# Four-pass graph network on one core: buffers reused after ScalarE's count of evictions instead of TensorE's count of sums

## What is computed

```
e = edges, s = src[e], d = dst[e]
1  score = exp(clip(sum_over_head(K[s] * Q[d] / sqrt(12) * E[e]), -5, 5));  x += sum_e(V[s] * score) / (sum_e(score) + 1e-6)
2  mean = sum_e(x[s]) / deg;  peak = max_e(relu(x @ Wpool + b)[s]);  x += leaky_relu(bn(x, mean) + bn(x, peak))
3  x += (sum_e(x[s] * ci[s]) * cj[d]) @ W + b
4  y = sum_e((x @ W)[s] * w[e]);  x += layernorm(y + bias) * gamma + beta
```

## Time and profile before

| what | us |
|---|---|
| median of 3 runs | 5184.86 (5175.81 to 5187.15) |
| profiled execution, first to last instruction (its own time is given by this span alone) | 5246.3 |
| GpSimd busy | 3200.4 (61%) |
| TensorE busy, matrix products | 2714.9 (52%) |
| VectorE busy | 1982.1 (38%) |
| ScalarE busy | 1353.8 (26%) |
| gathers of pass 1, first to last | 42.0 to 1411.5 |
| gathers of pass 2 | 1471.2 to 2718.4 |
| gathers of pass 3 | 2809.2 to 3998.5 |
| gathers of pass 4 | 4024.9 to 5214.0 |

### The profile page before, as it was taken

One profiled execution on the slowest core, in us unless ns is written; L12 is line 12 of the kernel. 1 busy time (PEld: TensorE's weight loads), 2 busy tenths in 40 slices (PEclk: granted clock), 3 DMA queues, 4 the chain that ended last, 5 costly groups with the idle time before them and its releaser, 6 DMA issues.

```text
span 5246.3 us, 56090 instructions
## 1 busy us (share of the span) xinstructions
PE 2714.9 (52%) x15042; PEld 2473.5 (47%) x15042; DVE 1982.1 (38%) x4498; ACT 1353.8 (26%) x4318; POOL 3200.4 (61%) x3366
## 2 busy tenths in 40 slices
PE   6666676666756666566683543332334333333334
PEld 6666676666645555556552432222224222222234
DVE  3555545555655555555554111111113221122124
ACT  1121112222333333333343321211112121111113
POOL 4555555556356666666646666666665666666664
PEclk7676666767777777777785555555555555555555
DMA  7655555555433333333321111111112111111111
GB/s 193 156 142 140 148 137 139 149 143 144 125 94 85 81 84 83 82 83 83 83 60 42 35 35 35 35 35 35 35 35 46 35 36 34 35 35 34 35 35 44
DMA packets 337349, 409.90 MB, mean 78 GB/s; under 512 B 212224, under 2 KB 248691, under 8 KB 336957
## 3 DMA queue, kind: packets, MB, share of 16 engines
q0 software_dynamic: 133120, 245.58, 19.7%
q1 hardware_dynamic: 203933, 160.75, 11.7%
HBM read 386.26 MB, written 19.77 MB: 77 GB/s over the span
## 4 chain that ended last, share of the span: by engine, by line
another core or an unknown queue 32%; PE 19%; DVE 15%; POOL 14%; issue 14%; ACT 3%; DMA 1%; SPq 1%; ACTq 0%; DVEq 0%; POOLq 0%
POOL rows L563 14%; PE bank L655 10%; DVE same L1557 3%; DVE first_only L1256 2%; PE bank L669 2%; DVE first_only L1395 2%; DVE same L1256 2%; PE bank L668 1%; DVE prod L1325 1%; DVE score L1327 1%; DVE prod L1323 1%; PE bank L752 1%; DVE first_only L1264 1%; PE bank L759 1%
## 5 line engine op out<-in xcount | busy, mean ns | idle before, releaser
L655 PE MATMUL bank<-same,rows 128*96 128x128 f32 x4992 | 1059.8, 385 | 1468.8 <-issue 540.6
L655 PEld LDWEIGHTS bank<-same,rows 128*96 128x96 f32 x4992 | 917.5, 246 | 1593.7 <-issue 866.8
L563 POOL DMA_INDIRECT rows<-kv_table,src_idx x832 | 789.7, 949 | 610.0 <-DVE msg L1335 357.0
L563 POOL DMA_INDIRECT rows<-pair_table,src_idx x832 | 786.4, 945 | 520.5 <-issue 208.6
L563 POOL DMA_INDIRECT rows<-h_table,src_idx x832 | 788.7, 948 | 426.9 <-issue 235.0
L938 ACT COPY acc<-bank 96x511 f32 (+1 forms) x832 | 479.4, 576 | 2205.1 <-remote 1582.2
L563 POOL DMA_INDIRECT rows<-ci_table,src_idx x832 | 785.0, 943 | 412.6 <-issue 239.1
L1256 DVE TENSOR_TENSOR same<-bank,rank_col 128x512 f32<-128x512 f32 x624 | 420.6, 677 | 1000.7 <-remote 587.9
L1557 DVE TENSOR_SCALAR same<-iota_s,rank_col,src_hi 128x128 f32<-128x128 f32 x832 | 235.0, 359 | 906.7 <-remote 748.2
L655 PE MATMUL bank<-same,msg 128*105 128x128 f32 x1664 | 366.3, 391 | 384.5 <-ACT acc L940 362.7
L655 PEld LDWEIGHTS bank<-same,msg 128*105 128x105 f32 x1664 | 321.8, 268 | 398.2 <-DVE same L1256 200.9
(11 more groups left out here) (168 smaller groups left out, 2899.5 us busy)
## 6 DMA issues: line engine op xcount, KB each, us to landing
first_only<-in_attr_cols SPq DMA_DIRECT2D x104, 384.0 KB
first_only<-q_table SPq DMA_DIRECT2D x832, 48.0 KB
first_only<-rank_rows SPq DMA_DIRECT2D x104, 256.0 KB
first_only<-keep_rows SPq DMA_DIRECT2D x104, 192.0 KB
rows<-kv_table,src_idx POOLq DMA_INDIRECT x832
rows<-pair_table,src_idx POOLq DMA_INDIRECT x832
rows<-ci_table,src_idx POOLq DMA_INDIRECT x832
rows<-h_table,src_idx POOLq DMA_INDIRECT x832
```

Of the source, the lines that this page charges most:

```text
L563: pool.indirect_dma_start(rows[:, k, j, 0:width], None, table, bass.IndirectOffsetOnAxis(ap=src_idx[:, t:t + 1], axis=0)).then_inc(rows_in ...
L655: mm = pe.matmul(out[0:nrow, here], left(j), right(j), start=(j == 0), stop=(j == TQ - 1), skip_group_check=True)
```

## The change

Three waits of GpSimd and six of VectorE name another count. No instruction is added or removed, and the values waited for are the same.

```diff
-            edge_pass_pool(pool, pair_table, PAIR, passes[1].agg_done)
+            edge_pass_pool(pool, pair_table, PAIR, passes[1].copied)
...
-            edge_pass_pool(pool, ci_table, F, passes[2].agg_done)
+            edge_pass_pool(pool, ci_table, F, passes[2].copied)
...
-            edge_pass_pool(pool, h_table, F, passes[3].agg_done)
+            edge_pass_pool(pool, h_table, F, passes[3].copied)
...
-                    wait(dve, s0.agg_done, q - 1)
+                    wait(dve, s0.copied, q - 1)
                     one_hot(same[:, k % 2], iota_over, rank_col, q, P).then_inc(s0.same_done.sem, 1)
...
-                    wait(dve, s1.agg_done, q - 1)
+                    wait(dve, s1.copied, q - 1)
                     one_hot(same[:, k % 2], iota_over, rank_col, q, P).then_inc(s1.same_done.sem, 1)
-                    wait(dve, sel_done, q - 1)
+                    wait(dve, max_copied, q - 1)
                     one_hot(last[:, k % 2], iota_over, rank_last, q, P).then_inc(last_done, 1)
...
-                    wait(dve, s2.agg_done, q - 1)
+                    wait(dve, s2.copied, q - 1)
...
-                    wait(dve, s3.agg_done, q - 1)
+                    wait(dve, s3.copied, q - 1)
```

## The result

| | us | |
|---|---|---|
| before | 5186.0 | median of 4 runs, 5175.81 to 5199.14 |
| after | 5329.03 | median of 4 runs, 5320.46 to 5342.83 |
| ratio | 1.0272 | 95% interval 1.0247 to 1.0296, so 143 us |

The change makes the kernel slower by 143 us. The forecast was 5422 us and the range 5195 to 5575: the direction and the range held, the forecast was 93 us too high. Its likeliest band, 5340 to 5500, missed the median by 11 us.

The account below looks back on a forecast made before the run. GpSimd was taken to bound the kernel, standing still for late `agg_done` counts. Its later restarts add 89 us (passes 3 and 4) and 148 (pass 2), VectorE 0: 5184.86 + 237 = 5422 us, range 5195 to 5575.

Parts of the forecast that it names:

- What bounds the kernel: All four passes: GpSimd, busy 785 to 790 us in each, is the engine to follow; its stops await `agg_done`.
- GpSimd, price of a restart: Passes 2 to 4: GpSimd restarts after L940, 0.82 us later a stop, 1.24 after two quads in pass 2.
- GpSimd, stops times price: Each stop's later restart is paid in full: 109 stops give +89 us in passes 3 and 4, 152 give +148 in pass 2.
- VectorE, `same` and `last`: VectorE's one-hot waits: 0 beside GpSimd's shift; `last` in pass 2 up to 0.6 us a quad beyond it.
- Pass 1: `same` has 1.46 us to spare after `copied` and GpSimd's wait isn't changed: 0, pass stays at 1369.5 us.
- ScalarE "becomes the last to speak": Passes 2 to 4: ScalarE signals last but is busy only 19 to 38%, running the same instructions.
- Only passes 3 and 4 pay: Pass 2 takes GpSimd's later restart from slack, passes 3 and 4 pay +89: 5274 us, chance 0.22.
- Nothing moves: Late counts come at times of their own, so GpSimd's next stop is 0.82 us shorter: 5185 us, chance 0.12.
- VectorE's chain takes over pass 2: The 1.43 us on `last` is paid in each quad, +297, plus 89 in passes 3 and 4: 5571 us, chance 0.10.
- Faster: Pass 2, GpSimd's wait at L560: a pause after each quad ends the 7.53 us standstills, -37: 5148 us, chance 0.06.
- The sum's base: The +237 us is added to the median 5184.86, not the profiled span 5246.3, which is 61 us above it.

Follow-up runs that it names:

- r1: Kernel before with only GpSimd's three waits (passes 2, 3 and 4) moved to the eviction counts, VectorE's as before: 5332.18 us, ratio 1.0265.
- r9: Kernel before with only GpSimd's and VectorE's waits of passes 3 and 4 changed, on the second chip: 4437.7 us against 4434.59, ratio 1.0005.
- r4_again: Kernel before, unchanged, run for a second profile on the first chip: 5189.4 us, profiled span 5187.6.
- r12: Kernel before with an extra ScalarE copy ahead of L938 and the changed waits in passes 3 and 4, second chip: 4435.13 us, ratio 1.0003.
- r2: Kernel before with only VectorE's six waits moved to the eviction counts, GpSimd's as before: 5215.41 us, ratio 1.0044.
- r3: Kernel before with only pass 2's three waits changed (GpSimd's, `same`, `last`): 5293.86 us, ratio 1.0164.

## Why the prediction was right, and by how much it was off

**What bounds the kernel: right for the chip that was measured.** GpSimd's standing still is the lever, and its three waits carried the loss (r1). That the counts are late on one of two chips only, neither the trace of one profile nor the prediction could tell: on the second chip the same forecast would have been wrong, as GpSimd has no stop there to lengthen (r9). That the result came from a chip with late counts was luck.

**GpSimd, price of a restart: right.** The prediction had +0.82 us, and +1.24 for a long stop. From the count's arrival to GpSimd's start the trace of after has 1.12 us in passes 3 and 4, and 1.12 or 1.53 in pass 2, against 0.26 before: +0.86 and +1.27. What stands ahead of the eviction in the long case is another step than the one named: the maxima were evicted at 1592.08, before GpSimd stopped, and L1031 came first.

**GpSimd, stops times price: the step that failed.** "If the next batch of counts comes a set time after GpSimd's next stop, nothing makes this up" gave +89 for passes 3 and 4 and +148 for pass 2. Measured, against the second profile of before: +42 and +99.5. The premise, that the counts come a set time after GpSimd stops whether one quad or two were gathered before, was a misreading of the earlier trace rows. VectorE's start at 2199.93 is that of `last`, which waits for `sel_done` (L1388), not for the `agg_done` of GpSimd. GpSimd's own stops tell of its own count: 1.34 us after one quad and 2.21 after two there, and in pass 3 of the same profile 2.61 after three (restart at 2883.61) and 4.5 after six. So the time from the stop to the count was never a set one; it was longer where more quads had been gathered. Nor does each late count wait for a stop. In pass 3 of before, a sum that ends at 3584.1 is followed in the midst of a run of gathers:

```profile
3590.68 0.69 DVE L1256 TENSOR_TENSOR same<-bank,rank_col 128x512 f32<-128x512 f32 x1 [10.59 <-remote]
3590.73 0.94 POOL L563 DMA_INDIRECT rows<-ci_table,src_idx  x1 [0.30 <-remote]
```

In passes 2 to 4 of r4_again ScalarE had to wait for 287 counts that came over 1 us after their sum's modelled end; 140 of them came during a stop of GpSimd.

So a later restart changes the rhythm, and its price is not simply added. In pass 2 two quads went from 12.0 to 13.0 us where the change is paid most, 0.5 us a quad and not 0.82 or more. In pass 3 the period went from six quads with a stop of 4.5 us (first profile; the second has mostly pairs of stops there) to seven with one of 5.7, that is from 5.70 to 5.79 us a quad, where the forecast was 35.0 / 6 = 5.83. In pass 4 the forecast's 34.9 us a period came in the first 49 quads, and nearly the old 34.1 later. Another bound from r4_again: in its passes 2, 3 and 4 there are 196, 66 and 56 quads whose gather started earlier than 0.27 us after the L940 in question, by 186, 57 and 46 us in sum. Paid in full that is 289 us; 141 were paid, about half. Why TensorE's counts come as they do, and so why about half is worked off, stays open: r12, meant to isolate it, met a chip without late counts.

**VectorE, `same` and `last`: 0 beside GpSimd's shift, right** (r1 against the whole change). Alone they cost 0.44% (r2), all in pass 2, which the prediction had only as "up to 0.6 us a quad" beyond GpSimd's shift; 25 / 208 is 0.12.

**Pass 1: 0, right as far as it can be seen.** On the first chip the pass took 1333 to 1370 us in seven profiles with the old wait on `s0` and 1341 to 1356 in three with the new one.

**ScalarE "becomes the last to speak": right, and under-used.** The chain that ended last after the change is 10% ScalarE and 1% GpSimd, where r4_again has 5% and 9% (over a third of the chain has no name in either); before, had GpSimd restart ahead of L940.

**The rivals.** Only passes 3 and 4 pay: refuted by r3. Nothing moves: refuted on the first chip, and what happened in each kernel that ran on the second, though for another reason than that rival gave (no stop to shift, rather than a rhythm set elsewhere). VectorE's chain takes over pass 2: refuted. One of its signs did come, `last` starting on ScalarE's count of maxima (463 us of VectorE's waits in the pass). But r1 has the same length without VectorE's edits, GpSimd's mean stop grew by 1.1 us (320.1 / 116 against 1.66) and not by over 1.3, and the granted clock, 0.79 before and 0.77 after, didn't fall towards the 0.53 of the later passes. By the rule that stood beside that rival, from the Trainium skill (TensorE: Matmul & The Clock Gate, "HAM oscillation — how this bites in real kernels"), idle gaps between groups of products lower the clock. The trace agrees in direction at most: TensorE's idle time in the pass went from 466 to 504 us (its window less its busy time) and the clock fell by 0.02. Faster: refuted; the pause did not come after each quad but grew after every second one.

**The sum's base.** The prediction started from the median instead of the long profile, which was right: r4_again put the largest part of the excess, 25 us, in pass 1.

## What to carry to other kernels

Moving a wait from the producer's count to that of its consumer costs something only where the waiter restarts before the step that it will wait for has ended. Whether it does can be read ahead, as the waiter's start minus the end of that step (here, as the median of pass 2, -0.6 us on one chip and +10.4 on the other; in passes 3 and 4 of the first chip the median was positive, and the 30% of quads below 0.27 made the loss). How much it costs could not be read ahead: stops times price gave 237 us, the sum of the shortfalls 289, and the runs 143, since a later restart changed the rhythm itself. Ask also what the consumer has queued ahead of that step: ScalarE's L1031 stood before the eviction. Before you read when a count arrives from a follower's start, check that this follower waits for that count. And where followers idle long after their producer's modelled end, run the kernel on another chip before you tune the wait: what was tuned here doesn't exist there.

## What the runs showed of the hardware that was not expected

- **Late TensorE counts on one chip.** On the first chip VectorE, ScalarE and GpSimd see TensorE's count up to some 16 us after the modelled end of the products (15.6 in the earlier trace rows); on the second VectorE starts 0.03 us after it. Counts of ScalarE arrive within 0.03 us at VectorE and 0.27 at GpSimd on the first chip too. The whole kernel takes 5193 us on the one and 4435 on the other, 15% less, at the same 0.95 us a gather. Why is open, also whether the products themselves end late or only their count. Three, four or eight places made no difference, and the product behind the sum of 3004.96 did not bring its count out.
- **Pass 1 is longer on the first chip as well**, though GpSimd waits for VectorE there: 1344 us against 1075.
- **The extra 0.58 us of ScalarE in each quad is free** where counts are timely: 416 more copies, 1.0004 (0.9995 to 1.0014).
